# Who makes the sums and differences of the gate and up weights: GpSimd instead of the vector engine

## The reference

```python
x = x + xattn(layernorm(x), ctx, Wq, Wk, Wv, Wskip)
Wg, Wu, Wd = (dequantize(W_q, scale, zero) for gate, up, down)   # (nibble - zero) * scale, groups of 64
g, u = x' @ Wg.T, x' @ Wu.T          # x' = layernorm(x), 2752 hidden units
x = x + (silu(g) * u) @ Wd.T
```

## Time and profile before

| | |
|---|---|
| median of three runs | 1484.96 us (1483.7 to 1485.29) |
| the profiled execution: time, span | 1484.24 us, 1481.9 us |
| PE busy | 1454.1 us, 98% of the span |
| DVE busy | 820.8 us, 55% |
| ACT busy | 637.5 us, 43% |
| POOL busy | 207.2 us, 14% |
| granted TensorE clock, mean | 0.995 of full |

### The profile page before, as it was taken

One profiled execution on the slowest core, in us unless ns is written; L12 is line 12 of the kernel. 1 busy time (PEld: TensorE's weight loads), 2 busy tenths in 40 slices (PEclk: granted clock), 3 DMA queues, 4 the chain that ended last, 5 costly groups with the idle time before them and its releaser, 6 DMA issues.

```text
span 1481.9 us, 18688 instructions
## 1 busy us (share of the span) xinstructions
PE 1454.1 (98%) x6774; PEld 716.3 (48%) x6774; DVE 820.8 (55%) x1175; ACT 637.5 (43%) x1189; POOL 207.2 (14%) x265
## 2 busy tenths in 40 slices
PE   6999999999999999999999999999999999999998
PEld 5666665444444444444444444444444444444443
DVE  4788886834644544544554554554554463563265
ACT  5888884344243343333433433424433333433320
POOL 1233232011011011011101101101101101101100
PEclk8999999999999999999999999999999999999999
DMA  5222222157548547638638638637737737737794
GB/s 161 85 97 97 81 87 71 44 103 153 100 84 165 105 71 170 113 59 181 113 57 175 119 48 169 118 64 155 129 57 155 133 61 148 139 57 156 133 335 171
DMA packets 47028, 174.82 MB, mean 118 GB/s; under 512 B 6672, under 2 KB 9488, under 8 KB 42640
## 3 DMA queue, kind: packets, MB, share of 16 engines
q0 software_dynamic: 23040, 83.90, 34.6%
q1 hardware_dynamic: 23808, 90.20, 20.1%
q10 hardware_dynamic: 144, 0.26, 0.0%
HBM read 73.67 MB, written 100.66 MB: 118 GB/s over the span
## 4 chain that ended last, share of the span: by engine, by line
PE 95%; DVE 2%; issue 1%; ACT 1%; POOL 0%; DVEq 0%; POOLq 0%
PE ps L505 51%; PE ps L561 28%; PE ps L467 3%; PE ps L434 3%; PE ps L668 2%; PE ps L462 2%; PE ps L651 2%; PE ps L456 2%; PE ps L422 1%; DVE neg_max L1041 1%; ACT temps L706 1%; PE ps L410 0%; PE ps L412 0%; DVE xt L1046 0%; DVE xt L1417 0%
## 5 line engine op out<-in xcount | busy, mean ns | idle before, releaser
L505 PE MATMUL ps<-xt,w_gu 128*128 128x512 f16 x3528 | 789.1, 379 | 0.0
L505 PEld LDWEIGHTS ps<-xt,w_gu 128*128 128x128 f16 x3528 | 345.2, 98 | 414.9 <-issue 0.6
L561 PE MATMUL ps<-w_d_all,h_all 128*128 128x512 f16 x1920 | 440.5, 379 | 0.0
L817 ACT ACTIVATE stage<-ps,pow 128x512 f32<-128x512 f32 x320 | 220.0, 687 | 413.5 <-PE ps L561 413.5
L561 PEld LDWEIGHTS ps<-w_d_all,h_all 128*128 128x128 f16 (+1 forms) x1920 | 187.8, 98 | 226.6
L382 POOL DMA_DIRECT2D out<-stage x160 | 139.0, 868 | 1029.1 <-ACT stage L817 1029.1
L1182 DVE TENSOR_TENSOR temps<-ps,temps 128x512 f32<-128x512 f32 x42 | 29.1, 692 | 210.9 <-PE ps L505 210.9
L804 ACT CAST h_all<-temps 128x512 f16<-128x512 f32 x42 | 25.8, 614 | 131.0 <-DVE temps L1201 131.0
L1187 DVE TENSOR_TENSOR temps<-ps,temps 128x512 f32<-128x512 f32 x42 | 29.1, 692 | 95.0 <-PE ps L505 95.0
L1191 DVE TENSOR_TENSOR temps<-ps,temps 128x512 f32<-128x512 f32 x42 | 29.0, 690 | 75.7 <-PE ps L505 75.7
L1195 DVE TENSOR_TENSOR temps<-ps,temps 128x512 f32<-128x512 f32 x42 | 29.0, 689 | 75.1 <-PE ps L505 75.1
(11 more groups left out here) (114 smaller groups left out, 1283.4 us busy)
## 6 DMA issues: line engine op xcount, KB each, us to landing
out<-stage POOLq DMA_DIRECT2D x160, 512.0 KB, 5.3
grid<-grids SPq DMA_DIRECT2D x136, 256.0 KB, 4.9
raw<-packed SPq DMA_DIRECT2D x22, 512.0 KB, 3.7
out<-stage SPq DMA_DIRECT2D x17, 512.0 KB, 2.9
stage<-x SPq DMA_DIRECT2D x13, 512.0 KB, 3.6
raw_d<-packed SPq DMA_DIRECT2D x12, 512.0 KB, 7.9
xt<-out SPq DMA_DIRECT2D x12, 512.0 KB, 11.0
out<-xt SPq DMA_DIRECT2D x12, 512.0 KB, 2.6
```

What stands on the lines that cost most here:

```text
L505: mm = pe.matmul(bank, w_gu[e][:, wp, w, P * j:P * j + P], xt[:, xb, xp, j, cols], start=(fresh and n == 0), stop=(n == 3 * J - 1), skip_g ...
L561: mm = pe.matmul(ps[:, 6 + oh, :], h, w, start=(n == 0), stop=(n == len(products) - 1))
L817: act.activation(stage[:, t % STAGES, NOUT * oh:NOUT * oh + NOUT], ps[:, 6 + oh, :], ACT.Copy, scale=pow2[:, 10:11]).then_inc(s_stage, 1)
```

## The change

The sums of all pairs leave DVE's queue and are put into POOL's. The set in the attention stage stays where it was. Twenty sets of four move; the operations, their tiles and their semaphores are the same, and the waits for `s_weight_lo` and `s_comb` move with them.

```diff
             for n in range(XROWS):
                 pool.wait_ge(s_store[n], 16 * len(range(n, B, XROWS)))
-            for d in range(B * PAIRS):
-                add_tile(d, d % B)
+            q, r = quant[:, :].bitcast(F32), raw[:, :].bitcast(F32)
+            q0, q1, r0_, r1 = q[:, 0:512], q[:, 512:1024], r[:, 0:512], r[:, 512:1024]
+
+            def first_sums(lo, comb):
+
+                pool.wait_ge(s_weight_lo, lo + 2)
+                pool.tensor_tensor(r1, q1, r1, ALU.add).then_inc(s_comb, 1)
+                pool.wait_ge(s_comb, comb + 1)
+                pool.tensor_tensor(q1, q0, q1, ALU.subtract).then_inc(s_comb, 1)
+
+            def second_sums(comb):
+
+                pool.wait_ge(s_comb, comb + 2)
+                pool.tensor_tensor(q0, r1, q0, ALU.subtract).then_inc(s_comb, 1)
+                pool.wait_ge(s_comb, comb + 3)
+                pool.tensor_tensor(r0_, r0_, q0, ALU.subtract).then_inc(s_comb, 1)
+
+            first_sums(4, 4)
+            second_sums(4)
+            for p in range(PAIRS):
+                add_tile(B * p, 0)
+                first_sums(10 * p + 10, 8 * p + 8)
+                add_tile(B * p + 1, 1)
+                second_sums(8 * p + 8)
+                for t in range(2, 11):
+                    add_tile(B * p + t, t)
+                if p + 1 < PAIRS:
+                    first_sums(10 * p + 14, 8 * p + 12)
+                    second_sums(8 * p + 12)
+                for t in range(11, B):
+                    add_tile(B * p + t, t)
@@ second_up_and_down(p), DVE
-                    if at == 0:
-                        first_sums(10 * p + 4, 8 * p + 4)
-                        second_sums(8 * p + 4)
                     if at == 1:
                         mixed_lo(1, 10 * p + 4)
@@ next_up(p), DVE
                     if at == 1:
                         plain_lo(0, 10 * p + 10)
-                    if at == 2:
-                        first_sums(10 * p + 10, 8 * p + 8)
-                    if at == 3:
-                        second_sums(8 * p + 8)
                     if at == 5:
                         mixed_lo(0, 10 * p + 10)
```

## The result

The kernel after took 1488.64 us, the median of 13 runs (1486.3 to 1490.92), against 1484.96 us for 13 runs of the kernel before (1483.0 to 1487.34) on the same chip. The ratio is 1.0025, with a 95% interval of 1.0017 to 1.0034: 3.7 us slower. My forecast was 1485.6 us, and my range ended at 1488.5. The profiled span is 1485.8 us, against 1481.9.

A forecast was written before the change was run, and what follows sets the result against it. PE was taken to bound the kernel, so DVE relief gains 0; later pairs cost 0 and the first pair 0.6 us, giving 1484.8 us from the profiled 1484.24 and 1485.6 from the median, range 1483.5 to 1488.5 us.

The forecast's parts named there:

- PE bounds the stretch: From 240 to 1400 us PE works end to end with one 1.0 us wait, so relieving DVE gains 0.
- The sums on POOL: A set of four chained sums on POOL takes 5.9 us, at most 9.8, against some 2.9 on DVE.
- place one: Instance 4p+1 of a pair, where one of its two sets of four sums is made after plain_lo.
- Contention, 0.9 us on the chain of place one: In instance 4p+1, h1_out and lo1 on DVE each delay POOL's sums by 0.45 us, giving a 6.8 us chain.
- h1_out or lo1 keep their length: Sign against the forecast: these DVE instructions, run beside POOL's sums, were expected to take longer.
- the other set: The sums of instance 4p+3: no DVE instruction with two SBUF operands beside them, so no contention was charged.
- Place one and place two cost 0: In instances 4p+1 and 4p+3 of later pairs, POOL's sums come early enough that PE loses nothing.
- First pair, 0.6 us once: Without down tiles, the first pair's second mixed_lo starts 1.0 us late; PE stands about 0.6 us, up to 3.6.
- the rival "absorbed": The change moves nothing in effect, as the first pair absorbs its 0.6 us too: 1485.0 us, chance 0.12.
- The 0.39 us that DVE had to spare: DVE's slack before L1187 at 269.83 us in the first pair, taken off the 1.0 us lateness.
- m1_copy near 280 us: End of the first pair's delay path: m1_copy at 279.38 us, which PE's weight load at 280.00 awaits without slack.
- The sum, 0 + 0.6: Total cost: 0 for later sets at both places plus 0.6 us for the first pair; forecast 1485.6 us.

The follow-up runs named there:

- slow_one: after_pad128 with one idle POOL tensor_tensor ahead of each of the four sums: 1488.48 us, ratio 1.0023.
- slow_two: after_pad128 with two idle POOL tensor_tensor operations ahead of each of the four sums: 1531.79 us, ratio 1.0309.
- after_pad22: The changed kernel with 22 one-column memsets added to DVE's queue in instance 41, where DVE idles: 1484.63 us, ratio 1.0000.
- after_pad34: The changed kernel with 34 narrow memsets added to DVE's queue in instance 41: 1483.7 us, ratio 0.9994.
- before_pad12: The kernel before, sums on DVE, with 12 narrow memsets added to DVE's queue in instance 41: 1482.87 us, ratio 0.999.
- after_pad21: The changed kernel with 21 narrow memsets added to DVE's queue in instance 41: 1490.94 us, ratio 1.0038.
- after_again: The changed kernel once more, in a new build and with nothing else altered: 1488.39 us, ratio 1.0023.
- place_two_only: The changed kernel with the sums of instance 4p+1 back on DVE, only those of instance 4p+3 on POOL, no padding: 1488.21 us, ratio 1.0022.
- after_pad128: The changed kernel with 128 narrow memsets added to DVE's queue in instance 41: 1482.46 us, ratio 0.9984.
- before_pad106: The kernel before, sums on DVE, with 106 narrow memsets added to DVE's queue in instance 41: 1483.0 us, ratio 0.9991.

## Why the prediction was wrong

- **PE bounds the stretch, and the 55 us taken off DVE give back nothing.** Right: 114.00 of 114 us on both sides.
- **The sums on POOL.** A little too long: undisturbed sums took 1.27 us behind gaps of 0.08, so a set without contention is 5.3 us where I had 5.9, and with it 5.7 us at place one where I had 6.8. All sums lay between 1.27 and 1.77 us.
- **Contention, 0.9 us on the chain of place one.** Half right. POOL paid 0.4 us on the first sum, beside h1_out, and DVE's lo1 paid 0.3, 1.02 us where 0.68 is usual (708.94 us). I had named "h1_out or lo1 keep their length" as a sign against me: h1_out did keep it (0.74). Nobody waited for either. In the first pair POOL paid nearly all of the 0.9: 1.62 and 1.77 us for the sums beside h1_out and lo1. Beside the other set I had said that there was none, yet its first and third sum took 1.59 and 1.57 us, each straight behind an add's DMA; why is open.
- **Place one and place two cost 0.** Right. slow_one and slow_two bear out the cover, with 2.5 us per sum hidden and 3.9 not.
- **First pair, 0.6 us once.** Wrong, and small: it is the rival "absorbed". In after the fourth sum ended at 266.57, and DVE's second mixed_lo started at 267.68 where 267.2 would have been the old place (266.43 + 0.75). It was 0.5 us late, and not 1.0: the chain took 6.2 us where I had 6.8, by the shorter sums and gaps and not by less contention. The 0.39 us that DVE had to spare at the earlier trace rows took nearly all of it: PE's row runs from 260.02 for 39.06 us after and from 259.27 for 39.03 before. PE has no wait near 280 us. For a longer delay the path was wrong too: PE first meets u2_out, not m1_copy near 280 us. In slow_one the second mixed_lo is 4.3 us late (271.45, the trace lying 0.7 us later) and PE waits 2.8, in slow_two 9.8 and 8.3: 1.5 us of cover in both, not the 0.4 that I had.
- **The sum, 0 + 0.6.** This is the step that failed. It has no term for the code behind the loop, which puts that code at nothing without a reason. I wrote that I read the waits of PE "from 240 to 1400 us, the whole stretch in which the change acts". The change acts on DVE's queue as a whole: it takes 22 instructions out of it, and the first block boundary behind the loop moves from one point of the tail to another. The term is +2.0 us of wait, and about 1 us of clock in the profiled execution, against a measured 3.7. The remaining 0.7 us are no larger than what the start varies by, and I leave them open. The clock bears on them: seven of the 13 executions of after ran at a mean granted clock of 0.993 or less, and took 1489.5 us in the mean, the other six 1487.4; no execution of before in the later sets lay under 0.994. That the missing term is the layout and nothing that the sums do is shown by after_pad22 (sums on POOL, no loss), after_pad34 and before_pad12 (the boundary at the same place, the same tail of 46.0 us in both) and after_pad21 (sums untouched, 5.8 us).

Could it have been foreseen? The sign could: the row of 2.11 us ahead of tile 7 stood in the profile before, charged to a PE that had nothing left to do for that tile, in a row of adds with pauses of mostly 0.26 to 0.48 us, and the order of the instructions gave the 22. With the packets of the instruction queue beside it, a stop at tile 14 could be worked out. Its length of 4.2 us, twice the old one, could not.

What stays open: why the first packet starts sooner or later by the place within three instructions, and so why the stop has the length that it has; why the clock is lowered behind some of these waits and not behind others of the same length (after and after_again are one kernel); and why the medians of after_pad21 and place_two_only lie 5.9 and 3.2 us above before, where the tails of their profiled executions give 3.8 and 1.0. The other executions have no trace, but their mean granted clock is on record: eight of the eleven of place_two_only ran at 0.993 or 0.994 and took 1488.7 us in the mean, the profiled one at 0.996 and 1483.0. So a lower clock goes with the longer times. Whether it fell behind the wait, how much of the time it is, and what a later start adds, isn't shown.

## What to carry to other kernels

A change that adds or removes instructions on an engine shifts all that comes behind them in its queue, also far from the place where it acts. Look in the profile before for pauses marked "issue", or charged to an engine that had already finished, near packets of an instruction queue, count the instructions that the change removes, and see where the pause slides to. Before a difference of a few tenths of a per cent is put down to the work that was moved, run the changed kernel with as many idle instructions put back as were taken out. Where the code behind a loop ends the kernel, it can pay to put padding where the engine is idle, so that the first load falls there: here 128 narrow memsets gave 5.9 us over the changed kernel and 2.6 over the one before, both measured beside it.

## What the runs showed of the hardware

DVE's instructions come in packets of 8 KB over q14: its packets in the tail move with DVE's padding (1457.5 us in before, 1446.5 with 12 memsets more). The same queue has others that move with POOL's work: in the pairs, behind 302 us, two in after_pad128 (347.0 and 941.3 us) and four in slow_one (312.3 to 1418.8, one of these in the tail). In every kernel whose tail was read the first boundary behind the loop stopped DVE: 2.1, 3.0 or 4.2 us at a tile by its place in the three instructions, 3.8 to 4.0 ahead of the second add of tile 3, and 2.6 to 2.7 among memsets. From the start of the first packet to DVE's next instruction it was 1.7 to 1.9 us each time. The boundary after it cost PE 0.2 us at most where it could be seen (before_pad106, after_pad128). The Trainium skill ("Runtime: NRT & Kernel Launch", section "Instruction fetch mechanics") says that instructions come in blocks of 16 KiB, that crossing a boundary costs "one DMA tail-bump, mostly hidden", and that a taken branch breaks the sequential prefetch. In these traces the packets of q8 have 16 KB and those of q14 8 KB. The second boundary agrees with "mostly hidden". The first does not, and the measurement decides: a loop that has just been left is the case nearest to its words on branches, but no run here takes the loop away, so that the loop is the reason is argued and not shown.

An undisturbed idle tensor_tensor of 128x512 on POOL took 1.04 us (slow_one, reading one operand twice) and a sum of two operands 1.27, up to 1.77 beside DVE, and 1.57 to 1.59 straight behind an add's DMA in the pair that was read.
